# Half taps and small statistics taken by turns in tile 3 of a directional convolution

## The reference

```python
def _gn(v, G=32, eps=1e-5):
    g = v.reshape(B_, G, C_ // G, H_, W_)
    m = jnp.mean(g, axis=(2, 3, 4), keepdims=True)
    s = jnp.var(g, axis=(2, 3, 4), keepdims=True)
    return ((g - m) / jnp.sqrt(s + eps)).reshape(v.shape)

def _L0_conv_ref(x, dw_weight, pw_weight, pw_bias):
    h = jax.lax.conv_general_dilated(x, dw_weight, window_strides=(1, 1),
                                     padding=((1, 1), (1, 1)), feature_group_count=C)
    h = jax.nn.gelu(h, approximate=False)
    maps = jnp.einsum('bchw,oc->bohw', h, pw_weight) + pw_bias[None, :, None, None]
    maps = maps.reshape(B, DIRS, C, H, W)
    out = jnp.zeros_like(x)
    for i, (dx, dy) in enumerate(OFFSETS8):
        diff = jnp.roll(x, shift=(dy, dx), axis=(-2, -1)) - x
        out = out + maps[:, i] * diff
    return out

x = x + _L0_conv_ref(_gn(x), ...)
```

## Time and profile before

| what | value |
|---|---|
| median of three runs | 2215.76 us |
| lowest and highest | 2214.11 and 2215.88 us |
| the profiled execution's own time | 2214.68 us |
| its span, first to last instruction | 2212.9 us |
| PE busy | 2158.2 us, 98% |
| DVE busy | 2067.0 us, 93% |
| POOL busy | 1978.2 us, 89% |
| ACT busy | 1839.9 us, 83% |
| granted TensorE clock | 0.999 of full |

### The profile page before, as it was taken

One profiled execution on the slowest core, in us unless ns is written; L12 is line 12 of the kernel. 1 busy time (PEld: TensorE's weight loads), 2 busy tenths in 40 slices (PEclk: granted clock), 3 DMA queues, 4 the chain that ended last, 5 costly groups with the idle time before them and its releaser, 6 DMA issues.

```text
span 2212.9 us, 28734 instructions
## 1 busy us (share of the span) xinstructions
PE 2158.2 (98%) x10769; PEld 2019.3 (91%) x10769; DVE 2067.0 (93%) x2234; ACT 1839.9 (83%) x2762; POOL 1978.2 (89%) x857
## 2 busy tenths in 40 slices
PE   1999999999999999999999999999999999999998
PEld 1999999999999999999999999999999999999998
DVE  7999999999999999999999999999999999999996
ACT  5979889798887988889788897988879888797775
POOL 5799899899989999899898998999989998999985
PEclk9999999999999999999999999999999999999999
DMA  6245264443725437254462644536354372543424
GB/s 183 48 79 129 48 113 99 89 103 51 157 52 107 92 60 159 34 109 100 70 139 35 124 98 81 114 50 131 79 94 98 60 164 35 108 101 51 100 34 75
DMA packets 47083, 202.13 MB, mean 91 GB/s; under 512 B 3040, under 2 KB 7136, under 8 KB 45664
## 3 DMA queue, kind: packets, MB, share of 16 engines
q0 software_dynamic: 30192, 94.97, 26.3%
q1 hardware_dynamic: 16752, 105.34, 18.6%
HBM read 104.88 MB, written 146.80 MB: 114 GB/s over the span
## 4 chain that ended last, share of the span: by engine, by line
PE 84%; DVE 11%; ACT 2%; issue 2%; DMA 0%; POOL 0%; SPq 0%; DVEq 0%; ACTq 0%
PE psum L922 84%; DVE psum L775 4%; DVE products L702 3%; DVE psum L702 1%; ACT psum L587 1%; DVE psum L784 1%; ACT psum L555 1%; DVE acc L724 1%; ACT hid L569 1%; DMA acc<-x 0%; DVE acc L756 0%; POOL hlo L332 0%; DVE mean_b L678 0%; DVE psum L679 0%; DVE fields L807 0%
## 5 line engine op out<-in xcount | busy, mean ns | idle before, releaser
L587 ACT ACTIVATE psum<-psum,bias,rstd 128x448 f32<-128x448 f32 x1792 | 1200.1, 694 | 323.7 <-PE psum L922 320.5
L922 PE MATMUL psum<-hhi,w_hi 128*128 128x448 f32 x3601 | 1301.9, 362 | 47.0 <-ACT hhi L574 45.3
L363 POOL TENSOR_TENSOR acc<-acc,products 128x896 f32<-128x896 f32 x333 | 1165.8, 3501 | 162.1 <-DVE products L702 150.0
L922 PE MATMUL psum<-hhi,w_lo 128*128 128x448 f32 x3584 | 1300.2, 363 | 0.0
L922 PE MATMUL psum<-hlo,w_hi 128*128 128x448 f32 x3584 | 1009.0, 363 | 0.3 <-POOL hlo L332 0.3
L784 DVE SCALAR_TENSOR_TENSOR psum<-xn,dw_f,psum 128x896 f32<-128x896 f32 x768 | 881.3, 1148 | 72.3 <-ACT psum L559 66.7
L922 PEld LDWEIGHTS psum<-hhi,w_hi 128*128 128x128 f32 x3601 | 676.7, 188 | 97.0 <-issue 45.3
L922 PEld LDWEIGHTS psum<-hlo,w_hi 128*128 128x128 f32 x3584 | 673.2, 188 | 44.9 <-POOL hlo L332 0.9
L922 PEld LDWEIGHTS psum<-hhi,w_lo 128*128 128x128 f32 x3584 | 673.4, 188 | 43.9
L702 DVE TENSOR_TENSOR products<-psum,fields 128x896 f32<-128x896 f32 x555 | 600.6, 1082 | 14.7 <-ACT psum L587 11.1
L332 POOL TENSOR_TENSOR hlo<-hid,hhi 128x896 fp32r<-128x896 f32 x112 | 264.5, 2362 | 12.8 <-ACT hhi L574 12.8
(11 more groups left out here) (67 smaller groups left out, 448.2 us busy)
## 6 DMA issues: line engine op xcount, KB each, us to landing
out<-acc POOLq DMA_DIRECT2D x96, 896.0 KB, 7.7
out<-x SPq DMA_DIRECT2D x16, 3136.0 KB, 12.9
xpad<-x SPq DMA_DIRECT2D x30, 1568.0 KB, 14.8
out<-acc POOLq DMA_DIRECT2D x15, 448.0 KB, 5.6
acc<-x SPq DMA_DIRECT2D x4, 784.0 KB, 6.7
xpad<-pw_t SPq DMA_DIRECT2D x1, 2048.0 KB, 12.1
out<-products SPq DMA_DIRECT2D x2, 224.0 KB, 1.9
dw_f<-dw SPq DMA_DIRECT2D x1, 9.0 KB, 8.1
```

What stands on the lines that cost most here:

```text
L363: nc.gpsimd.tensor_tensor(a, a, p, ALU.add).then_inc(added_s, 1)
L587: nc.scalar.activation(m, m, ACT.Identity, bias=bias[ip][:, g, d:d + 1], scale=rstd[ip][:, g:g + 1]).then_inc(biased_s, 1)
L922: last = nc.tensor.matmul(maps(n0 * UNITS + q)[:, side, x0:x1], w[:, kk, col:col + P], h_part(h, t, nl, kk)[:, x0:x1], start=s == 0, stop= ...
```

## The change

Three things are done. In group_stats the difference of the moments and their mean was computed twice, into dev_t (PSUM) and dev_s (SBUF), and the two were multiplied; now it is computed once, into dev_s, and dev_s is multiplied by itself. STAT is 10 instead of 11. In tile 3 half taps become single items: a new function half_tap makes one, and the branch for them leaves tap. And the order in front of the third product becomes a turn of one small statistic and one half tap, three times, with the next statistic between the product and its addition and one half tap behind that.

```diff
-        STAT = 11
+        STAT = 10
...
-                then(nc.vector.tensor_tensor(dev_t, mom_t[:], mean_t, ALU.subtract))
                 then(nc.vector.tensor_tensor(dev_s[:], mom_t[:], mean_t, ALU.subtract))
                 yield
                 wait()
-                then(nc.vector.tensor_tensor(dev_t, dev_t, dev_s[:], ALU.mult))
+                then(nc.vector.tensor_tensor(dev_t, dev_s[:], dev_s[:], ALU.mult))
...
+            def half_tap(n0, b0, c, j, g):
+
+                conv, ky, kx = conv_of(n0, c), *divmod(TAPS_DVE[j], 3)
+                if j == 0:
+                    dve.wait_ge(start_s, upto(START_OF, b0, c) + (g + 1))
+                else:
+                    dve.wait_ge(tap_s, upto(TAPS_OF, b0, c) + (2 * (j - 1) + g + 1))
+                d = conv[:, g, :].rearrange("p (r c) -> p r c", c=W)
+                nc.vector.scalar_tensor_tensor(
+                    d, xn[c % 2][:, g * TR + ky:g * TR + ky + ROWS, kx:kx + W],
+                    dw_f[:, g, TAPS_DVE[j]:TAPS_DVE[j] + 1], d, ALU.mult, ALU.add).then_inc(tap_s, 1)
...
                     def tap_next():
                         for j in itertools.islice(taps, 1):
                             tap(n0, b0, nl + 3, j)
+                        half_tap_next()
+                        half_tap_next()
...
-                    stats_next()
-                    stats_next()
-                    tap_next()
-                    stats_next()
-                    second_product(n0, nl)
-                    second_add(n0, nl)
-                    stats_next()
-                    tap_next()
+                    if single:
+                        stats_next()
+                        half_tap_next()
+                        stats_next()
+                        half_tap_next()
+                        stats_next()
+                        half_tap_next()
+                        second_product(n0, nl)
+                        stats_next()
+                        second_add(n0, nl)
+                        half_tap_next()
+                    else:
+                        tap_next()
+                        second_product(n0, nl)
+                        second_add(n0, nl)
+                        tap_next()
```

More of the change, by code:

```diff
@@ L767, in tap @@
                 ky, kx = divmod(TAPS_DVE[j], 3)
[L768 to L778, removed]
                 if j == 0:
@@ L850, in body, with half_tap_next @@
                     t, par = nl % TILES, nl // TILES
-                    taps = iter(range(NT) if not (last and nl + 3 >= STEPS) else ())
+                    single = (nl + 3) % CSTEPS == SINGLE
+                    taps = iter(range(NT) if not single and not (last and nl + 3 >= STEPS) else ())
+                    half_taps = iter(itertools.product(range(NT), range(HALVES)) if single else ())
+                    def half_tap_next():
+                        for j, g in itertools.islice(half_taps, 1):
+                            half_tap(n0, b0, nl + 3, j, g)
                     def tap_next():
@@ L863, in body @@
                     first_product(n0, nl, 1)
+                    assert single == (t == STATS_TILE)
                     if t == STATS_TILE and not (last and par):
                         stats = iter(group_stats(b0 + par + 1))
-                    stats_next()
-                    stats_next()
-                    tap_next()
-                    stats_next()
-                    second_product(n0, nl)
-                    second_add(n0, nl)
-                    stats_next()
-                    tap_next()
+                    if single:
[14 more added lines that the diff above has]
+                        tap_next()
                     stats_next()
```

## The result

The changed kernel takes 2227.62 us, the median of five runs (2227.18 to 2228.21), against 2215.54 for the kernel before in five runs (2214.11 to 2215.88). The ratio is 1.0056, with a 95% interval of 1.0045 to 1.0068: 12.1 us slower. Forecast were 2230.2 and +14.4.

The account below looks back on a forecast made before the run. TensorE was taken to bound the kernel, with VectorE close behind. Port waits of 14.5 us over 15 images, less 0.1 in the start, made +14.4, so 2230.2 us on the median; whole range 2208.5 to 2235.

Parts of the forecast that it names:

- What bounds the kernel: TensorE, 98% busy, stalls 0.38 us in tile 4 of 15 images because product 7 is 0.27 late; 6.0 us to win.
- The walk along tile 3: VectorE in tile 3: product 2 starts 0.18 later, its addition's delay is covered, the multiplication is due 0.60 us earlier.
- The port wait as the upper bound: Tile 3: the multiplication with two SBUF inputs waits for the rest of GpSimd's hlo subtraction, to about its end; chance 0.70.
- Its size: Product 3 later by 0.97 us in one image, 1.25 in seven and 0.68 in seven: 14.5 us in all.
- The start: One small statistic less on VectorE in front of the taps: -0.1 us, without a port wait, as GpSimd is idle.
- The signs: Profile after: multiplication about 1.3 to 2.1 us in 15 of 16 runs, ending with GpSimd's subtraction; PE stops twice an image.
- No port wait: Rival: tile 3's multiplication runs in 0.1 us and the stall goes, -6.0 - 0.1, 2209.7 us; chance 0.22.
- a short wait: Rival: VectorE gets in at a seam of GpSimd's work after about 0.3 to 0.9 us; 2211 to 2220; chance 0.08.
- Product 2 too late: Rival: single half taps cost 0.13 more each, the addition misses unit 5 of tile 3, nothing is won; within the 0.08.

Follow-up runs that it names:

- the lower cluster: Version with turns and two differences, but four half taps before product 2 and none behind its addition: five of eleven times, from 2213.1 to 2214.4 us.
- the first experiment: The changed kernel with the difference computed twice again, into PSUM and SBUF, and the multiplication with one PSUM operand: 2208.62 us, ratio 0.9973 to the kernel before.

## Why the prediction was right, point by point

- **What bounds the kernel.** Right: with the turns and a PSUM operand the stall in tile 4 is gone and 6.05 us with it (6.0 said). Against 2208.6, two half taps in front took 2.5 more (2.9 said), and four, in the lower cluster, 4.5 to 5.8 (4.8 said), so the stop does follow from how late the product or the addition is, plus about 0.11.
- **The walk along tile 3.** Right to about 0.01 us: the multiplication 5.33 behind the transpose, product 2 without idle time in front of it, and the difference hidden in front of the addition.
- **The port wait as the upper bound.** Right in kind. Four kernels show it from four sides: without the second SBUF operand, with it in the old order, with a seam in GpSimd's work, with a second wait. The rule of the Trainium skill that I weighed (SBUF — State Buffer, Who interferes with whom) holds in the direction that no row of before had: the later one waits until the other's instruction is over (1.91 us instead of 0.19). What the runs show is this wait; that a shared port is behind it is the page's account.
- **Its size.** A little too large. The sum had product 3 start 0.10 behind the end of GpSimd's instruction; it starts 0.02 before it (256.19 and 256.21). So the images cost 1.13 and 0.57 instead of 1.25 and 0.68: 15 × 0.12 = 1.8 of the 2.3 us by which +14.4 was too much. The remaining 0.5 is within what two medians of this kernel differ by. The two traces differ by 13.4, but 0.8 of it lies before tile 3 of the first image, whose transpose is at 113.58 instead of 112.77.
- **The start.** The -0.1 is there, though no total can show it: from the transpose to the start of the last of the small statistics it is 1.97 us instead of 2.07 (16.95 to 18.92, and 16.59 to 18.66 before). The transpose itself is 0.36 later in the changed kernel's trace, with loads that landed later.
- **The signs.** As said, but for the multiplication's length of "about 1.3 to 2.1 us" in 15 of 16 runs: 14 are within it, one is 1.02.
- **The rivals.** No port wait, and a short wait of another kind: out, by the multiplication's 1.91 us and by the old order's loss. The time without a wait, 2209.7, was nearly that of the first experiment, 2208.6. Product 2 too late: it has the room that was read; only a fourth half tap uses it up.

## What to carry to other kernels

Before a duplicate operation is taken out, look at where its results lie: here the second copy in PSUM cost 0.1 us, hidden behind a product in the new order, and it kept a 32-column multiplication from waiting for an instruction of GpSimd's that takes 2.1 us. Where VectorE must have two SBUF operands beside a busy GpSimd, the price is the rest of GpSimd's current instruction, so GpSimd's instructions near it should be short, or it should meet a gap. The best safe version here is the one with the turns and two differences, 2208.6 us; the cut matmul should stay, since a stop of PE would otherwise risk the slow pace to the end.

## What the runs showed of the hardware that I had not expected

- TensorE has two steady paces for the same matmuls at the same granted clock: 0.200 and 0.207 us each. The slow one may begin where PE has waited for a product, if only for 0.01 us, and it lasted until a matmul of 448 columns was cut into two of 224 or another such wait came; in one execution it went from image 0 to the end, some 60 us in all. The "some images in which the gap is a little longer" of the prediction were this: in 4 of 15 images the unit behind the stop, in front of the cut, takes 2.57 or 2.58 us instead of 2.51.
- A stop of PE costs about 0.11 us more than the wait itself: the second matmul behind it starts 0.31 after the first.
- GpSimd gives way at the seam even between two instructions that follow each other at once. But the meeting is a matter of 0.1 us: a multiplication that came 0.09 before the start of GpSimd's next instruction took 0.20 us, one that came 0.05 behind such a start waited for all of it.
